# Second cross attention of a four-layer network: Fourier transforms split by even and odd frequencies, halves folded on GpSimd, the way back on two row strips, normalising on ScalarE

## The reference, cut to what matters

```python
def _L1_xattn_ref(queries, keys, values, wq, wk, wv, wo):      # 16 heads of Dh = 16
    Q, K, V = (queries @ wq, keys @ wk, values @ wv)           # each to (batch, head, Dh, L)
    corr = irfft(rfft(Q) * conj(rfft(K)), n=Lv)                # over the L = 256 tokens
    top_vals, top_idx = jax.lax.top_k(corr, 5)
    w = jax.nn.softmax(top_vals, axis=-1)
    t = jnp.arange(Dh)
    for i in range(5):
        gather_idx = (t[None, None, :] - top_idx[..., i]) % Dh
        out = out + w[..., i, None] * take_along_axis(V, gather_idx[..., None], axis=2)
    return out @ wo

x = x + tanh(g_xattn[1]) * _L1_xattn_ref(_layernorm(x), ctx_1024, ctx_1024, wq, wk, wv, wo)
```

## Time and profile before

| | us |
|---|---|
| median of three runs | 3182.99 |
| the profiled execution | 3189.49 |
| its span | 3187.8 |
| TensorE busy | 2882.6 (90%) |
| VectorE busy | 1698.4 (53%) |
| ScalarE busy | 1198.5 (38%) |
| GpSimd busy | 504.8 (16%) |

### The profile page before, as it was taken

How to read it: one execution, slowest core, us unless ns; L and a number is a source line. 1 busy time by engine, 2 the same in 40 slices (tenths; PEclk the granted TensorE clock), 3 DMA queues, 4 the chain that set the end, 5 groups by cost and what they waited for, 6 DMA issues and landing times. The chain is left out here.

```text
span 3187.8 us, 57727 instructions
## 1 busy us (share of the span) xinstructions
PE 2882.6 (90%) x20755; PEld 2294.8 (72%) x20756; DVE 1698.4 (53%) x4456; ACT 1198.5 (38%) x2275; POOL 504.8 (16%) x819
## 2 busy tenths in 40 slices
PE   7969999999998998999799689999799989857998
PEld 6856666666665787788687556666588877756998
DVE  4537777777774011677675478777322237741111
ACT  1315555555553121444334335444333223322221
POOL 1101111111110000000454401110000001032111
PEclk9979999999998999999799889999899999958999
DMA  3010000000000543000224410000111100064553
GB/s 117 0 34 2 1 0 0 0 0 0 0 0 1 171 146 127 20 20 13 93 75 141 123 38 27 20 20 1 62 53 53 53 19 0 0 226 146 179 178 130
DMA packets 109918, 182.34 MB, mean 57 GB/s; under 512 B 17004, under 2 KB 82668, under 8 KB 103408
## 3 DMA queue, kind: packets, MB, share of 16 engines
q1 hardware_dynamic: 99920, 155.55, 15.5%
q0 software_dynamic: 9888, 25.38, 2.2%
HBM read 149.14 MB, written 33.59 MB: 57 GB/s over the span
## 5 line engine op out<-in xcount | busy, mean ns | idle before, releaser
L507 DVE TENSOR_REDUCE m0hnm<-banks 128x4 f32<-128x1024 f32 x256 | 313.0, 1222 | 172.9 <-PE banks L435 172.7
L534 ACT ACTIVATE m0hpT<-banks 128x1024 f32<-128x1024 f32 x256 | 262.8, 1027 | 355.2 <-PE banks L448 355.2
L435 PE MATMUL banks<-m0hk,m0hq 32*128 32x256 f32 x2048 | 292.4, 403 | 12.1 <-DVE m0hnm L507 11.7
L448 PE MATMUL banks<-m0hq,m0hk 32*128 32x256 f32 x2048 | 291.5, 401 | 1.1 <-ACT m0hpT L534 1.1
L532 ACT ACTIVATE a2hpT<-banks,a2hlow 128x512 f32<-128x512 f32 x256 | 162.0, 684 | 191.4 <-PE banks L448 191.4
L435 PEld LDWEIGHTS banks<-m0hk,m0hq 32*128 32x128 f32 x2048 | 175.8, 185 | 64.1 <-DVE m0hnm L507 33.2
L507 DVE TENSOR_REDUCE a2hnm<-banks 128x4 f32<-128x1024 f32 x128 | 156.6, 1223 | 87.9 <-PE banks L435 87.9
L448 PEld LDWEIGHTS banks<-m0hq,m0hk 32*128 32x128 f32 x2048 | 177.7, 184 | 2.1 <-issue 1.7
L435 PE MATMUL banks<-a2hk,a2hq 32*128 32x256 f32 x1024 | 147.8, 406 | 21.9 <-DVE a2hnm L507 21.8
L2992 PEld LDWEIGHTS banks<-E3xT,E3w 128*128 128x128 f32 x1248 | 146.5, 195 | 4.3 <-issue 2.0
L2992 PE MATMUL banks<-E3xT,E3w 128*128 128x128 f32 x1248 | 148.7, 278 | 0.0
(11 more groups left out here) (469 smaller groups left out, 6386.8 us busy)
## 6 DMA issues: line engine op xcount, KB each, us to landing
E3w<-in_L_ffn_W_dram SPq DMA_DIRECT2D x47, 1024.0 KB, 20.7
E0w<-in_L_ffn_fw_dram SPq DMA_DIRECT2D x64, 512.0 KB
E2w<-in_L_ffn_w_dram SPq DMA_DIRECT2D x16, 1024.0 KB
E1xin<-slots SPq DMA_DIRECT2D x71, 130.0 KB
A2routed<-routed SPq DMA_DIRECT2D x16, 512.0 KB
slots_x<-E3zeros SPq DMA_DIRECT2D x1, 5070.0 KB, 23.9
E3xin<-slots_x SPq DMA_DIRECT2D x39, 130.0 KB
ctx_in<-in_ctx_dram SPq DMA_DIRECT2D x16, 256.0 KB
```

What stands on the lines that cost most here:

```text
L435: ins = pe.matmul(self.scores[:, j, tc], self.q[strip(half, j), u, e, c, chunk(tc)], self.k[strip(half, j), u, e, c], start=True, stop=True)
L448: ins = pe.matmul(self.turned[:, j, kc], self.k[strip(half, j), u2, e2, c2, chunk(kc)], self.q[strip(half, j), u2, e2, c2], start=True, st ...
L507: v.tensor_reduce(self.nm[:, e, :, at:at + 33:32].rearrange("p c g -> p g c"), self.scores, AX.X, ALU.max, negate=True).then_inc(self.nm_r ...
L534: ins = a.activation(dst, self.turned, ACT.Exp)
```

## The change

- **Transforms forward.** The 256 tokens are folded first: the sum of the two halves gives the even frequencies, their difference the odd ones. Each transform is then two half-sized ones, `halved`: for each of two chunks m and each parity e one matmul of 128 rows by 128 columns, written into alternate blocks of 64 columns of the bank. The folds are two adds or subtractions of 128 by 256 each, for x (`fold_x`, into xs) and for the context (`fold_c`, into cs), on GpSimd.
- **Transform back.** correlate splits the frequencies by parity over the partitions: even ones in rows 0 to 63, odd ones in 64 to 127, each parity into its own bank (4 and 6), so 8 matmuls of 64 rows and 128 columns. ScalarE copies the odd part (`take_odd`), and VectorE makes the two halves of corr as even plus odd and even minus odd.
- **Normalising** moves from VectorE to ScalarE (x times rstd plus shift), with shift computed on GpSimd in `norm`. In `take(b+1)` it stands between the copies of cw and of fq, for element b+2.
- **Order.** GpSimd's body(b) is fold_c(b+2), norm(b+2), fold_x(b+2). VectorE's stats(b+2) moves ahead of the wait for ex. SyncE's load of the context also waits for the fold that reads it. vw shares bank 5 with cw. At the stage's start dft_f and the context are loaded first, and stats, norm, apply and folds of elements 0 and 1 no longer wait for the weights. The two tables have half their size.

```diff
@@ -1210,30 +1210,34 @@
...
+        wq, wk, wv, wo = (sb(n, [P, C, D]) for n in ("wq", "wk", "wv", "wo"))
+        dft_f, dft_g = sb("f", [P, 2, P]), sb("g", [P, 2, P])
...
-        xn = sb("xn", [P, C, D])
+        xn, xs, cs = (sb(n, [P, C, D]) for n in ("xn", "xs", "cs"))
...
+        odd = sb("odd", [P, C, P])
...
+        st, mv, rstd, shift, absorb = (
+            sb("st", [P, C, 6]), sb("mv", [P, C, 2]), sb("rstd", [P, C]), sb("shift", [P, C]), sb("absorb", [P, C]))
...
+        co_banks = [bank(4), bank(6)]
@@ -1246,16 +1250,18 @@
 
         @block.sync
         def _(sp):
-            for t, n in ((dft_f, "dft_f"), (dft_g, "dft_g"), (wq, "L1_xattn_wq"), (wk, "L1_xattn_wk"),
-                         (wv, "L1_xattn_wv"), (wo, "L1_xattn_wo")):
+            cv = w["ctx_1024"].rearrange("b (c p) d -> b p c d", p=P)
+            sp.dma_start(dft_f[:], w["dft_f"]).then_inc(w_in, 16)
+            sp.dma_start(ctx_in[:], cv[0]).then_inc(c_in, 16)
+            for t, n in ((wo, "L1_xattn_wo"), (wq, "L1_xattn_wq"), (wk, "L1_xattn_wk"), (wv, "L1_xattn_wv")):
                 load_weight(sp, t[:], w[n], w_in)
+            sp.dma_start(dft_g[:], w["dft_g"]).then_inc(w_in, 16)
+            sp.dma_start(inner[:], w["inner"]).then_inc(w_in, 16)
             sp.dma_start(rot[:], w["rot"]).then_inc(w_in, 16)
             sp.dma_start(own[:], w["own"]).then_inc(w_in, 16)
-            sp.dma_start(inner[:], w["inner"]).then_inc(w_in, 16)
-            cv = w["ctx_1024"].rearrange("b (c p) d -> b p c d", p=P)
-            sp.dma_start(ctx_in[:], cv[0]).then_inc(c_in, 16)
             with sp.Fori(1, B) as b:
 
+                sp.wait_ge(cs_rdy, b)
                 sp.wait_ge(cw_mm, b)
                 sp.dma_start(ctx_in[:], cv[bass.ds(b, 1)].rearrange("b p c d -> p (b c) d")).then_inc(c_in, 16)
 
@@ -1266,29 +1272,51 @@
             def norm(b):
                 ch.start(b)
                 g.wait_ge(st_rdy, b + 1)
-                ln_rstd(g, ch, mv, rstd, env.mhalf, env.eps5).then_inc(rstd_rdy, 1)
+                ln_rstd(g, ch, mv, rstd, env.mhalf, env.eps5).then_inc(root_rdy, 1)
+                g.wait_ge(root_rdy, b + 1)
+                g.tensor_tensor(absorb[:], env.eps5[:], env.eps5[:], ALU.add)
+                for c in range(C):
+                    ins = g.tensor_scalar(shift[:, c:c + 1], mv[:, c, 0:1], rstd[:, c:c + 1], -1.0, ALU.mult, ALU.mult)
+                ins.then_inc(rstd_rdy, 1)
+
+            def halves(dst, src):
+
+                g.tensor_tensor(dst[:, 0], src[:, 0], src[:, 1], ALU.add)
+                return g.tensor_tensor(dst[:, 1], src[:, 0], src[:, 1], ALU.subtract)
+
+            def fold_x(b):
+                g.wait_ge(xn_rdy, b + 1)
+                if not (isinstance(b, int) and b == 0):
+                    g.wait_ge(fx_mm, b)
+                halves(xs, xn).then_inc(xs_rdy, 1)
+
+            def fold_c(b):
+                g.wait_ge(c_in, 16 * b + 16)
+                if not (isinstance(b, int) and b == 0):
+                    g.wait_ge(fc_mm, b)
+                halves(cs, ctx_in).then_inc(cs_rdy, 1)
 
             norm(0)
+            fold_c(0)
+            fold_x(0)
             norm(1)
+            fold_c(1)
+            fold_x(1)
 
             def body(b, one, two):
                 if two:
+                    fold_c(b + 2)
                     norm(b + 2)
+                    fold_x(b + 2)
             trailing(g, body)
 
         @block.vector
         def _(v):
             ch = Chain(v, v_ch)
-            EACH = 10
+            EACH = 11
 
             def stats(b):
                 ln_stats(v, ch, env.x[:, b], st, mv, env.scrap).then_inc(st_rdy, 1)
-
-            def apply(b):
-                v.wait_ge(rstd_rdy, b + 1)
-                if not (isinstance(b, int) and b == 0):
-                    v.wait_ge(fx_mm, b)
-                ln_apply(v, xn, env.x[:, b], mv, rstd).then_inc(xn_rdy, 1)
 
             def first(b):
                 v.wait_ge(fq_rdy, b + 1)
@@ -1299,20 +1327,23 @@
                 v.tensor_tensor(sp_[:, 0], ta[:, 0], ta[:, 1], ALU.add)
                 v.tensor_tensor(sp_[:, 1], tb[:, 0], tb[:, 1], ALU.subtract).then_inc(sp0_rdy, 1)
 
+            ch.start(0)
+            stats(0)
             for t in (corr, rep):
                 v.memset(t[:], -BIG)
             v.memset(mixT[:], 0.0)
+            v.wait_ge(xn_rdy, 1)
+            stats(1)
             v.wait_ge(w_in, 16 * loads)
-            ch.start(0)
-            stats(0)
-            apply(0)
-            stats(1)
             first(0)
-            apply(1)
 
             def body(b, one, two):
                 ch.start(EACH * b + 3 - (0 if one else 1))
-                v.wait_ge(co_rdy, b + 1)
+                v.wait_ge(odd_rdy, b + 1)
+                v.tensor_tensor(corr[:, :, 0:P], co_banks[0][:, :, 0:P], odd[:], ALU.add)
+                ins = v.tensor_tensor(corr[:, :, P:S], co_banks[0][:, :, 0:P], odd[:], ALU.subtract)
+                ch.link(ins)
+                v.sem_inc(co_rdy, 1)
                 v.memset(env.scrap[:], 0.0)
                 for c in range(C):
                     ins = v.max(top[:, c], corr[:, c, 0:S])
@@ -1323,6 +1354,9 @@
                 for c in range(C):
                     ins = v.match_replace(rep[:, c], top[:, c], corr[:, c], BIG)
                 ch.link(ins)
+                if two:
+                    v.wait_ge(xn_rdy, b + 2)
+                    stats(b + 2)
                 v.wait_ge(ex_rdy, b + 1)
                 for c in range(C):
                     ins = v.scalar_tensor_tensor(ex[:, c], rep[:, c, 0:S], BIG, ex[:, c], ALU.is_ge, ALU.mult,
@@ -1342,8 +1376,6 @@
                                           own[:].unsqueeze(2).broadcast_to([P, 8, KD]),
                                           mix[:, c].unsqueeze(1).broadcast_to([P, 8, KD]), ALU.mult)
                 ins.then_inc(blk_rdy, 1)
-                if two:
-                    stats(b + 2)
                 v.wait_ge(blkT_mm, b + 1)
                 for c in range(C):
 
@@ -1352,8 +1384,6 @@
                 ins.then_inc(mixT_rdy, 1)
                 if one:
                     first(b + 1)
-                if two:
-                    apply(b + 2)
                 v.wait_ge(o_mm, b + 1)
                 v.scalar_tensor_tensor(env.x[:, b], bank(7), env.tg[:, 1:2], env.x[:, b], ALU.mult, ALU.add).then_inc(x_rdy, 1)
                 if two:
@@ -1366,6 +1396,14 @@
                 a.wait_ge(mm, count)
                 a.activation(dst, bank(j), ACT.Copy).then_inc(done, 1)
 
+            def apply(b):
+                a.wait_ge(rstd_rdy, b + 1)
+                if not (isinstance(b, int) and b == 0):
+                    a.wait_ge(xs_rdy, b)
+                for c in range(C):
+                    ins = a.activation(xn[:, c], env.x[:, b, c], ACT.Identity, scale=rstd[:, c:c + 1], bias=shift[:, c:c + 1])
+                ins.then_inc(xn_rdy, 1)
+
             def take_fk(b):
                 a.wait_ge(fk_mm, b + 1)
                 a.activation(fk[:, 0], bank(3)[:, 0], ACT.Copy)
@@ -1375,22 +1413,31 @@
                 a.wait_ge(fg_rdy, b + 1)
                 a.activation(fg[0:1], bank(3)[0:1, 1], ACT.Copy).then_inc(fk_rdy, 1)
 
-            def take(b, between=None):
+            def take(b, between=None, ahead=None):
                 copy(fx_mm, b + 1, fx[:], 0, fx_rdy)
                 if between:
                     between()
                 copy(fc_mm, b + 1, fc[:], 1, fc_rdy)
                 copy(cw_mm, b + 1, cw[:], 5, cw_rdy)
+                if ahead is not None:
+                    apply(ahead)
                 copy(fq_mm, b + 1, fq[:], 2, fq_rdy)
                 take_fk(b)
                 if between:
                     a.wait_ge(o_mm, b)
-                copy(vw_mm, b + 1, vw[:], 6, vw_rdy)
+                copy(vw_mm, b + 1, vw[:], 5, vw_rdy)
+
+            def take_odd(b):
                 a.wait_ge(co_mm, b + 1)
-                a.activation(corr[:, :, 0:S], bank(4), ACT.Copy).then_inc(co_rdy, 1)
-
+                if not (isinstance(b, int) and b == 0):
+                    a.wait_ge(co_rdy, b)
+                a.activation(odd[:], co_banks[1][:, :, 0:P], ACT.Copy).then_inc(odd_rdy, 1)
+
+            apply(0)
+            apply(1)
             a.wait_ge(w_in, 16 * loads)
             take(0)
+            take_odd(0)
 
             def body(b, one, two):
                 def weights():
@@ -1399,21 +1446,30 @@
                         ins = a.activation(ex[:, c], corr[:, c, 0:S], ACT.Exp, bias=nmax[:, c:c + 1])
                     ins.then_inc(ex_rdy, 1)
                 if one:
-                    take(b + 1, weights)
+                    take(b + 1, weights, b + 2 if two else None)
+                    take_odd(b + 1)
                 else:
                     weights()
             trailing(a, body)
 
         @block.tensor
         def _(pe):
+            def halved(j, src):
+
+                for m in range(C):
+                    for e in range(2):
```

(71 more changed lines are left out.)

## The result

Beside each other on one chip the kernel before took 3182.52 us (median of 6 runs) and the changed one 3214.20 us (6 runs): ratio 1.0103, 95% interval 1.0081 to 1.0125. The forecast was slower, 3199; the direction and the mechanism held, but the loss is 31.7 us where the sum had +16.2. The profiled execution of the changed kernel is 3224.76 (span 3223.0) against 3189.49, +35.3. The stage itself, from its first load to the next stage's first, grew from 257.2 us (1268.34 to 1525.52) to 300.9 (1268.28 to 1569.14), +43.7. The other stages, whose code is the same, were 8.5 us shorter in sum in this one execution. Six runs of one kernel differ by up to 18.4 us (3207.76 to 3226.10), so this may be scatter; it is not shown. The length of the stage is the steadier measure: in a second profiled execution of the changed kernel it is 300.5.

A forecast was written before the change was run, and what follows sets the result against it. TensorE was taken as the bound (busy 199.88 of 201.50 us), with VectorE's chain nearly as long. Loop +23.0, last iteration -1.2, start -5.5, tail -0.1 made +16.2 on the median 3182.99: 3199 us, range 3184 to 3218.

The forecast's parts named there:

- the sum: All forecast terms for the whole kernel: +16.2 us, made against the profiled execution and added to the runs' median.
- The hold: ScalarE's apply waits for load, fold_c and norm, delaying fq and fk: period 16.0 against 14.39, +23.0 over 14 iterations.
- rival B: Correlate's strips don't overlap (1.78), or halved transforms cost more: +0.89 x 14, 3211 us; chance 0.08.
- rival C: TensorE's gaps lower its clock: up to +3.7 per iteration, 3250; once in three iterations, 3215; chance 0.13.
- rival A: The forecast itself, with bounds of load, folds and start: 3184 to 3211 us; chance 0.64.
- the full-size products ahead of the gap: Argument that TensorE's clock would not fall in the 2.6 us gap ahead of correlate; no size.
- the warning: GpSimd contends with VectorE's two-SBUF-input instructions, so folds beside them would cost more than 0.72 us each.
- If nothing else were late, 13.4: Period of the loop by TensorE's order and blk's readiness, without the new wait: 13.4 us, a clear gain.
- rival D: Load of ctx(b+2) and its folds release GpSimd early enough: period 13.4, 3162 us, faster; chance 0.08.
- the break-even: The sum shows no loss if the chain from load to correlate is 14.9 instead of 16.03, 1.1 us less.
- The start's -5.5: Stage start: TensorE begins 3.6 us earlier, fx to cw saves 1.9; together -5.5, bounds -3 and -7.
- The last iteration's -1.2: body(14), without apply or stats: blk at 9.27, correlate(15) at 13.2, so -1.2 us.

The follow-up runs named there:

- apply_late: Changed kernel with ScalarE's apply for b+2 moved behind the copies of fq and fk; 1.0000 of the kernel before.
- fold_twice: Changed kernel with two more adds of the same shape in fold_c, into a tile nobody reads; 1.0262 of the kernel before.
- gap_filled: Changed kernel with unread 128-column products in TensorE's waits, six before blk's and seven before correlate; 3181.95 against 3156.78 for the kernel before, 1.0079.
- small_after: Changed kernel with GpSimd folding only 8 columns of the context's halves from the third batch on; 1.0078 of the kernel before.
- after_again: Changed kernel without further edits, measured a second time; 3199.42 against 3160.01 for the kernel before, 1.0116.
- best: Changed kernel with apply after fk, GpSimd's norm ahead of fold_c, and TensorE's values product ahead of the wait for blk; 3147.13, 0.9963 of the kernel before.
- best_small: As best, but GpSimd folds only 8 columns of the context's halves from the third batch on; 3150.07, 0.9972 of the kernel before.
- best_ta: As best, with VectorE's ta product put ahead of its wait for the transposes; 3141.12, 0.9937 of the kernel before.

## Why the prediction was right, and where its sizes were off

**The hold** is right, and it is the main cause: shown by apply_late, which returns the whole loss, and borne out by fold_twice. In order, from correlate's start in the full-clock iteration:

- cw ends at 4.87 (forecast 4.56). 0.20 of it is correlate, whose 16 half-height instructions take 1.09 and not 0.89. The strips do run together, which rules out rival B (1.78), but not to the half that I took: an instruction costs 0.61 of a 128-row one (0.068 of 0.111). The row that I took it from the earlier trace rows, 0.143 against 0.216, said 0.66 by itself, which would have made 1.18. The first transform takes 0.99, the second 0.90.
- The load, from cw's end to GpSimd's fold, 2.87 (1422.35 to 1425.22). Forecast 2.9.
- fold_c 1.60 (forecast 1.44), since the second add takes 0.91 beside mixr. The first, which began 0.04 ahead of mixr, takes its 0.73. The bounds held.
- norm to ScalarE's start 2.02 (forecast 1.88): its first add takes 0.37 instead of 0.19 while mixr is still running.
- apply to the next correlate 5.22 (forecast 5.25).

0.31 - 0.03 + 0.16 + 0.14 - 0.03 = 0.55, the difference of 16.58 and 16.03, and over 14 iterations 7.7 us more than the sum had. This is the smaller of two mis-sized terms of the period.

**The clock** is the larger one. The sum gave it nothing, and rival C a chance of 0.13 with 1.2 per iteration in its mild form. It came: 1.31 per iteration in the profiled execution (18 us), and 14.5 to 14.8 us of the stage by gap_filled. The forecast's own rival A ended at 3211; that 3214 still lay in the range is due to the room left for B and for this mild form of C, not to the sum. My reason against it, "the full-size products ahead of the gap", was the step that failed. The earlier trace rows showed one idle stretch that left the clock at 1.00, and I read one row as a rule. The gaps also came out otherwise than forecast (1.6 ahead of the transposes, 2.6 ahead of correlate): 2.60 and 1.76 at a full clock, and behind a slow head up to 4.27 in one piece. The trace of the changed kernel holds gaps of 2.60 and 2.78 with the clock still up behind them and one of 2.98 with it down; in apply_late it fell behind one of 2.06, and in small_after behind one of 1.75. The Trainium skill, TensorE: Matmul & The Clock Gate (HAM oscillation), which told of a kernel whose waits lower its clock with each tile, described this case; the trace agrees, not at every iteration (ten of 14 in after_again) but at every one in fold_twice.

**GpSimd beside VectorE.** I left the warning unpriced. Its price is in the traces now: 0.42 becomes up to 0.95 to 1.0 for VectorE's 128x256 product, 0.73 becomes 0.90 to 0.99 for GpSimd's add, in best and best_small up to 1.23. So the traces agree with the Trainium skill, GPSIMD Engine Reference (Key points), that GpSimd contends with VectorE's instructions that have two SBUF inputs. On the forecast's chain it cost 0.3 per iteration; off it, it mattered more.

**"If nothing else were late, 13.4"**, on which rival D and the break-even rested, was too good. With apply moved the period is 14.2, and it took the two further reorderings of best_ta to come to 13.6. blk comes at 10.33 instead of 9.47: first max 0.21 later than I had it (2.56, as correlate is 1.09), 0.16 between max and weighting, 0.5 from the weighting to blk, through mixr beside the fold (1.29 for 0.76). A gap of 2 us ahead of the transposes follows, and the clock falls behind some of them. D's 3162 would hardly have come about even with a load that costs nothing.

**The ends.** The start's -5.5 measured -4.3. The first product came 0.7 later than forecast, because the 0.7 for fewer bytes was a misreading: the context was the tenth load before, so the wait was for 1.71 MB then as now, and it ended at 1276.54 before and at 1276.64 now. From cw to correlate(0) it took 9.62 instead of 9.05, which the sum did not have. The last iteration's -1.2 measured -1.4.

**What stays open:** why a gap of 2.8 lowers the clock in one iteration and not in another, and why it fell during one gap and 1 us or more behind another. That the dummy products cure it is shown; from which gap on it falls is not. What a second buffer for ctx_in would do, which would take the load off the chain, was not tried.

## What to carry to other kernels

When an in-order engine takes over a step of the element after next, follow that step's inputs back through every queue before counting what the move frees: here one apply, placed ahead of the copies of fq and fk, turned a load that had a whole period into a link of the chain. When work is taken from the bounding engine, re-sort its queue as well, so that what it can already do stands ahead of what it must wait for; otherwise the saving becomes a gap, and the gap can cost clock on top. And change a queue's order only against the bound of that kernel: the same move of the values product was worth -0.4% with the split and +0.5% without.

## What the runs showed of the hardware

- Empty stretches of 1.75 to 3.3 us on TensorE, behind full-size f32 products, brought the granted clock down to 0.50 in some iterations and not in others; those of 4.15 to 4.41 (six, in the two traces of the changed kernel) and of 5.5 to 5.8 (fold_twice) did in every one. It fell during the stretch or up to 1.7 us behind it (small_after: a stretch that ended at 1402.21, the clock 1.00 until 1403.8). Products of 128 columns at 1.16 then take 2.08, and full-size ones of 1.89 take up to 3.58.
- A GpSimd add of two SBUF tiles and a VectorE product of two SBUF tiles slow each other: 0.73 becomes 0.90 to 1.23, 0.42 becomes 0.95. Moving one such pair apart let the next pair meet.
- Even a GpSimd add of eight columns took 0.48 and 0.38 us beside VectorE's mixr, and 0.20 while VectorE waited (small_after, from 1426.90 and at 1394.99).
- Matmuls of 64 rows and 128 columns, alternating between two row strips and two banks, take 0.068 us each, where two at once at the pace of 128-row ones (0.111 each) would be 0.056.
